# Router and LoRA-A features of a conditional LoRA layer in plain fp32, with an earlier A load

## The reference

```
base   = x @ W.T                                  # 1024 x 1024, all in fp32
logits = x @ Wr.T + 5 * one_hot(language_id)      # 8 experts
gates  = softmax over the best 2 logits, 0 for the other experts
h      = x @ A.T                                  # 8 experts x rank 16 = 128 features
x1     = x + base + 2 * (h * gates) @ B           # layer 0
out    = x1 + x1 @ W1[adapter_id of the sequence].T   # layer 1, 16 adapters
```

## Time and profile before

| | us |
|---|---|
| median of three runs | 424.97 (424.17 to 424.98) |
| span of the profiled execution | 423.0 |
| PE busy | 414.4 (98%) |
| DVE busy | 314.1 (74%) |
| ACT busy | 163.1 (39%) |
| POOL busy | 59.5 (14%) |
| PE in the chain that ended last | 89% of the span |

### The profile page before, as it was taken

The page is one execution under the profiler, slowest core; times in us unless marked ns, Lnnn a source line. Parts: engine busy times, 40 slices in busy tenths (PEclk is TensorE's granted clock), DMA queues, the critical chain, the costliest instruction groups (busy, mean ns, idle before and its releaser), DMA issues.

```text
span 423.0 us, 6707 instructions
## 1 busy us (share of the span) xinstructions
PE 414.4 (98%) x1978; PEld 349.1 (83%) x1978; DVE 314.1 (74%) x378; ACT 163.1 (39%) x192; POOL 59.5 (14%) x104
## 2 busy tenths in 40 slices
PE   8898999999999999999999999999999999999996
PEld 8786888888898888888888888888889888888885
DVE  3999999999307999998615799999830799994410
ACT  3432544555212455454321445455421245533321
POOL 1021211201200121012110022111310012221000
PEclk9999999999999999999999999999999999999999
DMA  7994677797913666699650576679960356654111
GB/s 173 232 219 120 167 190 200 212 259 203 225 47 99 150 187 180 161 260 249 173 132 0 153 181 188 170 218 252 243 160 26 99 151 175 189 161 123 51 50 50
DMA packets 82542, 68.52 MB, mean 162 GB/s; under 512 B 7986, under 2 KB 82258, under 8 KB 82514
## 3 DMA queue, kind: packets, MB, share of 16 engines
q1 hardware_dynamic: 65618, 59.84, 55.3%
q10 hardware_dynamic: 16896, 8.39, 7.3%
HBM read 59.81 MB, written 8.39 MB: 161 GB/s over the span
## 4 chain that ended last, share of the span: by engine, by line
PE 89%; DVE 3%; DMA 2%; SPq 2%; issue 2%; ACT 0%; POOL 0%; DVEq 0%; ACTq 0%; POOLq 0%
PE banks L564 28%; PE banks L565 28%; PE banks L566 28%; PE banks L577 4%; SPq L255 2%; PE banks L579 1%; DMA raw<-in_L_cond_W_dram 1%; DMA raw<-in_x_dram 1%; DVE turned L349 1%; DVE turned L345 0%; DVE w_lo L356 0%; POOL raw L301 0%; PE gT_ps L611 0%; ACT w_hi L487 0%; DVE gT_lo L449 0%
## 5 line engine op out<-in xcount | busy, mean ns | idle before, releaser
L356 DVE TENSOR_TENSOR w_lo<-turned,w_hi 128x1024 fp32r<-128x1024 f32 x96 | 118.8, 1259 | 38.8 <-ACT w_hi L487 38.0
L487 ACT ACTIVATE w_hi<-turned 128x1024 fp32r<-128x1024 f32 x96 | 101.5, 1062 | 113.1 <-DVE turned L349 103.3
L349 DVE STREAM_TRANSPOSE turned<-raw 128x1024 f32<-128x1024 f32 x113 | 135.3, 1225 | 10.1 <-DMA raw<-in_x_dram 5.1
L301 POOL TENSOR_TENSOR raw<-raw,ident 128x128 f32<-128x128 f32 x96 | 58.4, 608 | 325.9 <-DMA raw<-in_L_cond_weight_dram 182.7
L564 PE MATMUL banks<-xT_hi,w_hi 128*128 128x512 f32 x256 | 100.2, 391 | 0.0
L565 PE MATMUL banks<-xT_lo,w_hi 128*128 128x512 f32 x256 | 99.7, 389 | 0.0
L566 PE MATMUL banks<-xT_hi,w_lo 128*128 128x512 f32 x256 | 99.6, 389 | 0.0
L564 PE MATMUL banks<-w_hi,x1T_hi 128*128 128x512 f32 x256 | 99.6, 389 | 0.0
L565 PE MATMUL banks<-w_lo,x1T_hi 128*128 128x512 f32 x256 | 99.6, 389 | 0.0
L566 PE MATMUL banks<-w_hi,x1T_lo 128*128 128x512 f32 x256 | 99.6, 389 | 0.0
L566 PEld LDWEIGHTS banks<-xT_hi,w_lo 128*128 128x128 f32 x256 | 48.1, 188 | 10.0
(11 more groups left out here) (54 smaller groups left out, 197.8 us busy)
## 6 DMA issues: line engine op xcount, KB each, us to landing
raw<-in_L_cond_weight_dram SPq DMA_DIRECT2D x256, 128.0 KB, 2.7
raw<-in_L_cond_W_dram SPq DMA_DIRECT2D x128, 128.0 KB, 3.5
raw<-in_x_dram SPq DMA_DIRECT2D x64, 128.0 KB, 3.3
out_dram<-out_stage ACTq DMA_DIRECT2D x32, 256.0 KB, 3.1
raw<-in_L_cond_A_dram SPq DMA_DIRECT2D x4, 128.0 KB, 3.1
raw<-in_L_cond_B_dram SPq DMA_DIRECT2D x4, 128.0 KB, 4.5
gated<-in_L_cond_Wr_dram SPq DMA_DIRECT2D x4, 8.0 KB
lang_i<-in_itok_B_dram SPq DMA_DIRECT2D x1, 4.0 KB, 2.9
```

The lines of the kernel that those rows point to most:

```text
L301: nc.gpsimd.tensor_tensor(spot, spot, ident[:].rearrange("p (q j) -> p q j", q=Q), ALU.add)\
L349: nc.vector.transpose(turned[:, slot(item, ch, last, 2)].rearrange("p m (q s) -> p q m s", q=Q), raw[:, s, :].rearrange("p (q m j) -> p q ...
L356: nc.vector.tensor_tensor(dest(False, item), turned[:, slot(item, ch, last, 2)], dest(True, item).bitcast(F32), ALU.subtract)\
L487: nc.scalar.activation(dest(True, item), turned[:, slot(item, ch, last, 2)], ACT.Copy)\
```

## The change

The features are no longer made of high and low parts: x, A and the router are multiplied in plain fp32. For that the transposed x of a chunk is kept in a buffer of its own (`x_turned`, four tiles), A is transposed straight into `fac`, and one matmul of 136 columns takes the place of the pair of 272 and 136. The gates read their logits and features from PSUM, so ScalarE's copy of `h` and VectorE's addition are gone (`GATE_STEPS` 9 for 10). A is loaded ahead of x, and the small loads (router, language ids, adapter ids) are issued by ScalarE. The features of the next chunk stand at the end of the loop body, and those of the first chunk ahead of the loop. There are two output buffers for four, and the small gate buffers and `gated` share memory with `wr_turned` and `x_turned`. x is still split into high and low parts for layer 0.

```diff
-    OUTS = 4
+    OUTS = 2
...
-    FIRST = [("x", 0), ("a", 0)] + [("x", j) for j in range(1, XT)] + [("w", 0), ("w", 1), ("w", 2), ("b", 0)]
+    FIRST = [("a", 0)] + [("x", j) for j in range(XT)] + [("w", 0), ("w", 1), ("w", 2), ("b", 0)]
...
-        fac = sb("fac", [P, M, 2, FC], F32R)
+        fac = sb("fac", [P, M, FC])
...
+        x_turned = sb("x_turned", [P, XT, M, P])
...
-        h = sb("h", [P, XT, FC])
-        gated = sb("gated", [P, XT, ER])
-        wr_raw = gated[:, 0:2, :].rearrange("p j f -> p (j f)")
+        gated = x_turned[:, 0, 0:XT, :]
+        wr_raw = x_turned[:, XT - 1, 0:2, :].rearrange("p m t -> p (m t)")
...
-        h_ps = banks[:, 0:XT, 0:2 * FC].rearrange("p j (s f) -> p j s f", s=2)
+        h_ps = banks[:, 0:XT, 0:FC]
...
+        def turned_tile(item, ch):
+            kind, n = item
             if kind == "a":
-                return fac[:, :, 0 if hi else 1, 0:ER]
-            return ring(w_hi if hi else w_lo, n)
+                return fac[:, :, 0:ER]
+            if kind == "x":
+                return x_turned[:, n]
+            if kind == "b":
+                return turned[:, AHEAD % 2]
+            return turned[:, n % 2 if ch is None else (n + 1) % 2]
...
             for item in FIRST:
                 load(item, None, False)
-                if item == ("x", 0):
-                    sp.dma_start(lang_i[:], lang_ids.partition_broadcast(P)).then_inc(lang_loaded, 16)
-                elif item == ("x", 1):
-                    sp.wait_ge(wr_zeroed, 1)
-                    for c in range(Q):
-                        sp.dma_start(wr_raw[c * S:c * S + E, :], wr[:, c * DQ:(c + 1) * DQ]).then_inc(wr_loaded, 16)
-                elif item == ("w", 0):
-                    sp.dma_start(adapters[:], adapter_ids.unsqueeze(0)).then_inc(adapters_loaded, 16)
...
+                if kind == "x" and ch is not None:
+                    dve.wait_ge(x_done, ch * XT + (n + 1))
+                    dve.wait_ge(h_ready, ch + 1)
...
-            make([x2, x3, first_w], None, False)
-            make(FIRST[6:-1], None, False)
+            turn(x3, None, False)
+            low(x2, None, False)
+            turn(first_w, None, False)
+            low(x3, None, False)
+            turn(FIRST[6], None, False)
+            low(first_w, None, False)
+            turn(FIRST[7], None, False)
+            low(FIRST[6], None, False)
+            low(FIRST[7], None, False)
...
-                dve.wait_ge(h_lo_copied, ch + 1)
-                nc.vector.tensor_tensor(h[:], h_ps[:, :, 0, :], h[:], ALU.add).then_inc(gate_steps, 1)
-                dve.wait_ge(gate_steps, at(1))
+                dve.wait_ge(h_ready, ch + 1)
...
-                                        h[:, :, 0:ER].rearrange("p j (e r) -> p j e r", e=E),
-                                        gates[:].unsqueeze(3).to_broadcast([P, XT, E, R]),
+                                        h_ps[:, :, 0:ER].rearrange("p j (e r) -> p j e r", e=E),
+                                        gates.unsqueeze(3).to_broadcast([P, XT, E, R]),
...
-            for item in FIRST[0:3]:
+            act.wait_ge(wr_zeroed, 1)
+            for c in range(Q):
+                act.dma_start(wr_raw[c * S:c * S + E, :], wr[:, c * DQ:(c + 1) * DQ]).then_inc(wr_loaded, 16)
+            act.dma_start(lang_i[:], lang_ids.partition_broadcast(P)).then_inc(lang_loaded, 16)
+            act.dma_start(adapters[:], adapter_ids.unsqueeze(0)).then_inc(adapters_loaded, 16)
+            for item in FIRST[1:-1]:
                 high(item, None, False)
...
-            def copy_h(ch):
-                act.wait_ge(h_ready, ch + 1)
-                nc.scalar.activation(h[:], h_ps[:, :, 1, :], ACT.Copy).then_inc(h_lo_copied, 1)
...
-                pe.wait_ge(fac_done, 2)
+                pe.wait_ge(fac_done, 1)
...
-                        nc.tensor.matmul(banks[:, j, 0:2 * FC], xT_hi[:, m, t],
-                                         fac[:, m, :, :].rearrange("p s f -> p (s f)"), start=m == 0, stop=False)
-                        mm = nc.tensor.matmul(banks[:, j, 0:FC], xT_lo[:, m, t], fac[:, m, 0, :],
-                                              start=False, stop=m == M - 1)
+                        mm = nc.tensor.matmul(banks[:, j, 0:FC], x_turned[:, j, m, :], fac[:, m, :],
+                                              start=m == 0, stop=m == M - 1)
...
-                    pe.wait_ge(gate_steps, ch * GATE_STEPS + 1)
+                    pe.wait_ge(gated_ready, ch + 1)
...
-                features(ch)
+                pe.wait_ge(x_done, ch * XT + XT)
...
+                if not last:
+                    features(ch)
+
+            features(None)
```

More of the change, by code:

```diff
@@ L190, in cond_resid_kernel @@
         setup = sem("setup")
-        GATE_STEPS = 10
+        GATE_STEPS = 9
         def place(item, ch, last):
@@ L317, in _, with same_tile_before @@
         def _(dve):
[L318 to L322, removed]
+            def same_tile_before(item, ch):
+                kind, n = item
+                if kind == "b":
+                    return [("w", AHEAD - 2)]
+                if kind != "w" or (ch is None and n < 2):
+                    return []
+                if ch is not None and n == AHEAD:
+                    return [("w", AHEAD - 1)]
+                if ch is not None and n == AHEAD + 1:
+                    return [("w", AHEAD - 1), ("b", 0)]
+                return [("w", n - 2)]
             def made(item, ch):
@@ L341, in turn @@
                     dve.wait_ge(raw_loaded[s], fills(item, ch, last) * (Q * 16))
-                for old in two_before(item, ch, last):
+                for old in same_tile_before(item, ch):
                     made(old, ch)
+                if kind == "x" and ch is not None:
+                    dve.wait_ge(x_done, ch * XT + (n + 1))
+                    dve.wait_ge(h_ready, ch + 1)
                 if kind == "b":
-                    nc.vector.transpose(turned[:, slot(item, ch, last, 2)].rearrange("p m (q k) -> p k q m", q=Q),
+                    nc.vector.transpose(turned_tile(item, ch).rearrange("p m (q k) -> p k q m", q=Q),
                                         raw[:, s, :].rearrange("p (e k r) -> p k e r", e=E // Q, r=R))\
@@ L348, in turn @@
                     return
-                nc.vector.transpose(turned[:, slot(item, ch, last, 2)].rearrange("p m (q s) -> p q m s", q=Q),
+                nc.vector.transpose(turned_tile(item, ch).rearrange("p m (q s) -> p q m s", q=Q),
                                     raw[:, s, :].rearrange("p (q m j) -> p q m j", q=Q, m=M))\
@@ L354, in low @@
                 kind, n = item
-                dve.wait_ge(hi_done, place(item, ch, last) + 1)
-                nc.vector.tensor_tensor(dest(False, item), turned[:, slot(item, ch, last, 2)],
+                dve.wait_ge(hi_done, split_before(item, ch, last) + 1)
+                nc.vector.tensor_tensor(dest(False, item), turned_tile(item, ch),
                                         dest(True, item).bitcast(F32), ALU.subtract)\
-                    .then_inc({"x": x_done, "w": w_done, "a": fac_done, "b": bT_done}[kind], 1)
+                    .then_inc({"x": x_done, "w": w_done, "b": bT_done}[kind], 1)
             def make(items, ch, last):
@@ L366, in make @@
                         low(before, ch, last)
-            x0, fac_a, x1, x2, x3, first_w = FIRST[0:6]
+            fac_a, x0, x1, x2, x3, first_w = FIRST[0:6]
+            turn(fac_a, None, False)
             turn(x0, None, False)
+            dve.wait_ge(wr_loaded, Q * 16)
+            nc.vector.transpose(wr_turned[:], wr_raw.rearrange("p (m j) -> p m j", m=M)).then_inc(wr_transposed, 1)
+            turn(x1, None, False)
+            dve.wait_ge(wr_transposed, 1)
+            nc.vector.tensor_copy(fac[:, :, ER:FC], wr_turned[:, :, 0:E]).then_inc(fac_done, 1)
+            low(x0, None, False)
             dve.wait_ge(consts, 3)
@@ L375, in _ @@
             nc.vector.tensor_copy(lang_f[:], lang_i[:]).then_inc(setup, 1)
+            turn(x2, None, False)
             dve.wait_ge(setup, 2)
@@ L378, in _ @@
                                     lang_f[:].unsqueeze(2).to_broadcast([P, NB, E]), ALU.is_equal).then_inc(setup, 1)
-            turn(fac_a, None, False)
-            low(x0, None, False)
+            low(x1, None, False)
             dve.wait_ge(setup, 3)
             nc.vector.tensor_scalar(bias[:], bias[:], LANG_BIAS, None, ALU.mult).then_inc(setup, 1)
[L383 to L390, removed]
-            make([x2, x3, first_w], None, False)
-            make(FIRST[6:-1], None, False)
+            turn(x3, None, False)
[7 more added lines that the diff above has]
+            low(FIRST[7], None, False)
             dve.wait_ge(setup, 4)
@@ L486, in high @@
                     act.wait_ge(w0_used, ch * M + M)
-                nc.scalar.activation(dest(True, item), turned[:, slot(item, ch, last, 2)], ACT.Copy)\
```

(9 more changed lines are left out.)

50 lines of the change are left out of this document (27 added, 23 removed).

## The result

The changed kernel is slower: 426.03 us (median of 13 runs, 424.62 to 426.49) against 424.31 us for the kernel before (13 runs), ratio 1.0029, 95% interval 1.0018 to 1.0041. I had forecast 424.1 against 424.97, which was the median of three runs. The profiled execution has a span of 424.4 us, against 423.0. Among the experiments one execution of the kernel before took 2393 us and one with 4 identity products 2409 us; they play no part in any ratio.

A forecast was written before the change was run, and what follows sets the result against it. TensorE's own work was taken to bound everything after the first LoRA product, with waits only at the start. From 424.97 us, 1.0 gained at the start and 0.15 lost on features gave 424.1; range 422.8 to 425.8.

The forecast's parts named there:

- The features: Feature matmuls of the three later chunks: 7.57 us a chunk against 7.52, taken as +0.15 us in three.
- two streams of the columns: Price of a plain fp32 feature matmul: two records, each two streams of 136 columns and 5 ns, 0.2367 us.
- bound by its weight load: Rival, 8%: a plain fp32 matmul costs 0.2234 us at any width, 1.1 us less on top of the start, 423.0.
- four passes: Reading of the warm-up's two records of 0.1117 us at 128 columns: plain fp32 takes four passes on TensorE.
- Two passes: Estimate from the skill page, not adopted: a feature step of 0.113 us, three chunks saving 11.7 us.
- Copies, output buffers, place of the features in the loop: Later chunks: removed copy and addition, two output buffers for four, and features at the loop's end change the time by zero.
- Base tile 0: First base tile on TensorE: begins at 23.5, later than 22.80, as its low part follows weight tile 1's turn on VectorE.
- Then 16.7 us without a stop: the LoRA product at 40.2.: First chunk on TensorE: three base tiles and transposes run unbroken to the first LoRA product, 1.0 us sooner than 41.20.
- The clock as a rival: Rival, 10%: idle TensorE before base tile 0 drops to half rate, losing 2.9 us; time 428.3.
- it decides from w1's landing: Condition for the clock's fall: second weight tile landing at 21.15 or later, base tile 0 at 24.8, array idle 4.3 us.
- my 3 us gap: Forecast idle time of TensorE between the first features' end at 20.5 and base tile 0, taken to cost no clock.

The follow-up runs named there:

- 4 identity products: Changed kernel plus 4 unneeded matmuls of the identity on TensorE between the first chunk's features and base tile 0: 425.26 us, ratio 1.0028 to the kernel before.
- at 68 columns: Changed kernel with the features of chunks 2 to 4 over 68 of 136 columns, good for times alone: 424.34 us, ratio 1.0009 to the kernel before.
- the exchanged order: Changed kernel with VectorE making the low part of weight tile 0 ahead of the turn of weight tile 1: 422.24 us, ratio 0.9954 to the kernel before.
- the longer wait: Kernel before, with base tile 0 waiting for the low parts of weight tiles 0 and 1: 428.18 us, ratio 1.0083 to the kernel before.
- 14 identity products: Changed kernel plus 14 unneeded matmuls of the identity on TensorE between the first features and base tile 0: 423.46 us, ratio 0.9976 to the kernel before.

## Why the prediction was wrong

The time of 426.03 lies above the range. Its base of 424.97 was 0.66 us above the 424.31 of 13 runs, so in the difference the miss is larger: 0.85 us gained were forecast, 1.72 us were lost. Point by point:

- **The features** (7.57 us a chunk, from 7.15 to 7.60, for 7.52): 7.41. The sign is off, by 0.16 us a chunk; that half of the instructions go and the time stays was right. The reason that I gave, two streams of the columns, is not: at 68 columns the price stayed. The case "bound by its weight load", to which I gave 8%, fits best, though it is inferred. It was worth 0.3 us in all and not 1.1, since at 136 columns the price is already 0.232 and not 0.223. So the two records of the earlier trace rows do not show four passes.
- **Two passes.** The Trainium skill's page Perfetto Trace Analysis, section Engine Utilization, gives fp32 in its low-high form half of the full rate; by the prediction's estimate from it 11.7 us would have gone. The trace does not agree: a matmul costs 0.232 us, not 0.113, and the three chunks gave 0.5 us.
- **Copies, output buffers, place of the features in the loop** at nothing: right; no wait of them shows in a chunk of 100.38 us.
- **Base tile 0** at 23.5 behind the turn of weight tile 1: it was 23.56. The second weight tile's addition ended 1.3 us sooner, at 21.05, as taken. In the other traces of this order base tile 0 began between 23.23 and 24.11, so to hit it within 0.1 us was partly luck.
- **"Then 16.7 us without a stop: the LoRA product at 40.2."** This is the step that failed. It was 43.16, since the first 13 matmuls ran at half rate. With the array kept busy it was 40.19, from 23.23 and 16.96 us in place of 23.5 and 16.7. So up to that product the other terms held to 0.3 us each, and the missing term was the clock's 1.8 to 2.9 us, which the forecast had put at nothing.
- **The clock as a rival**, 10%, "it decides from w1's landing" at 21.15 or later. The mechanism and the place were right, and its chance and its point were not. I compared my 3 us gap with one execution in which 1.9 us had cost nothing, and let that speak for 3 us. The clock fell behind 2.89 us with 4 identity products, so the gap of the forecast itself was already too long. The features also ended at 19.7 and not at 20.5, because the full clock had been granted sooner in that execution (the 37 warm-up products took 10.3 us in place of 11.25), so the gap was 3.8 us although the tile landed early. The rival's price of 2.9 us was the 2.9 of this profile, and 1.8 in the next.
- The Trainium skill's page TensorE: Matmul & The Clock Gate, section HAM oscillation — how this bites in real kernels, tells of a kernel in which each burst of matmuls behind a wait for data begins cold. Here the trace agrees, with 0.50 granted from 22.4 to 29.2. I had cited it and let one row overrule it.

## What to carry to other kernels

Before work is taken off the busiest engine, ask what idle stretch opens where that work stood: here features that ended sooner left the array idle, and the half rate of its next matmuls cost 1.8 to 2.9 us, more than the change brought. A few useless products, or better the operand that the array waits for made one step sooner, give it back; in an in-order queue, put the result that another engine waits for ahead of the preparation that still has to wait for its own data. And one execution in which a gap was harmless does not show that such gaps are: the mean granted clocks of the timed executions, sorted, tell how often a kernel loses it.

## What the runs showed of the hardware

- Idle stretches of TensorE and what followed: 1.45 us (the exchanged order) no fall; 1.76 us (the longer wait) a fall; 1.89 us in the kernel before none; 2.84 us (ahead of the features, in the longer wait), 2.89, 3.73, 3.84 and 4.71 us a fall each. Below 2 us the length alone does not decide: the 1.76 us came 5 us behind an earlier stretch at half rate, and 3 of 10 executions of the exchanged order lost clock.
- The half rate then lasted to 26.9 in one execution of the changed kernel and to 29.2 in another, for the same idle stretch: 1.8 and 2.9 us lost.
- Executions of one kernel differ. The mean granted clock was 0.996 or less in 25 of 25 of the changed kernel, in 17 of the 30 of the kernel before beside it, and in none of 12 with 14 identity products.
- A plain fp32 matmul leaves two records and costs 0.222 us at 68 columns, 0.223 at 128 and 0.232 at 136. That is hardly cheaper than two fp32r matmuls of 272 and 136 columns (0.235).
